# Four and two PSUM banks become three and three: the working ring and the score ring of an attention and mixture-of-experts layer

## The reference: what is computed

```python
x = x + _layernorm(_L0_attn_ref(_layernorm(x), Wq, bq, Wk, bk, Wv, bv))
x = x + _layernorm(_L0_ffn_ref(_layernorm(x), ...))

# attention: 8 blocks of 64 tokens; the first and the last block attend to all,
# block 1 to blocks 0, 1, 2, 7, block 6 to 0, 5, 6, 7,
# the others to block 0, block 7 and themselves with both neighbours
scores = einsum('bhqd,bhkd->bhqk', q, k) * 16 ** -0.5
ctx = einsum('bhqk,bhkd->bhqd', softmax(scores), v)

# feed-forward: a dense branch and 8 experts, the best two of each token
abel_out = gelu(xn @ abel_w + abel_b)
topw, topi = top_k(xn @ moe_gate_w + moe_gate_b, 2)
eo = gelu(xn @ ew1[e] + eb1[e]) @ ew2[e] + eb2[e]
moe_out = (weighted sum of eo) @ expm(gens[0]) @ expm(gens[1]) @ expm(gens[2])
gate = sigmoid(concat(abel_out, moe_out) @ gc_w + gc_b)
out = x + abel_out * (1 - gate) + moe_out * gate
```

## Time and profile before

| | |
|---|---|
| median of three runs | 1788.7 us |
| the profiled execution, its own time | 1799.32 us |
| its span in the profile | 1797.5 us |
| granted TensorE clock, mean | 0.953 of full |
| TensorE (PE) busy | 1543.8 us, 86% |
| weight loads (PEld) busy | 1062.6 us, 59% |
| VectorE (DVE) busy | 1228.8 us, 68% |
| ScalarE (ACT) busy | 898.9 us, 50% |
| GpSimd (POOL) busy | 705.7 us, 39% |
| start of step 3 and of step 15 of `front` | 212.7 us and 940.3 us of the span |

### The profile page before, as it was taken

One profiled execution on the slowest core, in us unless ns is written; L12 is line 12 of the kernel. 1 busy time (PEld: TensorE's weight loads), 2 busy tenths in 40 slices (PEclk: granted clock), 3 DMA queues, 4 the chain that ended last, 5 costly groups with the idle time before them and its releaser, 6 DMA issues. The chain is left out here.

```text
span 1797.5 us, 33500 instructions
## 1 busy us (share of the span) xinstructions
PE 1543.8 (86%) x10385; PEld 1062.6 (59%) x10386; DVE 1228.8 (68%) x3690; ACT 898.9 (50%) x1789; POOL 705.7 (39%) x716
## 2 busy tenths in 40 slices
PE   7889999999999999999999888399999999999500
PEld 5645555545554555455545556288888888888400
DVE  5667787788787878787888633356565665555287
ACT  3146766676667666766776553033333333333244
POOL 1011323442444335333542244144444444544377
PEclk9999999999999999999999989699999999999855
DMA  8132245335533543354334127645656656564397
GB/s 229 36 119 79 88 138 170 119 108 172 160 119 111 177 153 116 123 174 142 123 120 162 52 95 230 191 96 117 134 125 126 134 114 143 105 147 78 48 321 229
DMA packets 186637, 243.59 MB, mean 136 GB/s; under 512 B 23624, under 2 KB 157136, under 8 KB 186384
## 3 DMA queue, kind: packets, MB, share of 16 engines
q1 hardware_dynamic: 159632, 205.67, 36.5%
q0 software_dynamic: 26880, 36.33, 12.4%
HBM read 133.40 MB, written 105.91 MB: 133 GB/s over the span
## 5 line engine op out<-in xcount | busy, mean ns | idle before, releaser
L1053 ACT ACTIVATE pexp<-scT 128x512 f32<-128x512 f32 x768 | 433.6, 598 | 258.7 <-PE scT L839 256.1
L1240 DVE TENSOR_REDUCE mx<-work 128x1 f32<-128x320 f32 (+2 forms) x1024 | 500.6, 547 | 64.3 <-PE work L812 63.7
L1747 POOL DMA_INDIRECT y_rows<-rows_add,row_of x144 | 227.5, 1580 | 298.6 <-DMA y_rows<-rows_add,row_of 235.1
L839 PE MATMUL scT<-w 128*128 128x192 bf16 (+3 forms) x1536 | 282.1, 275 | 26.6 <-ACT pexp L1053 21.8
L812 PE MATMUL work<-w 126*128 126x320 bf16 (+4 forms) x1280 | 269.6, 295 | 31.0 <-DVE mx L1240 27.4
L1779 PE MATMUL h_ps<-inT,w1c 128*128 128x256 f32 x1152 | 263.5, 382 | 2.4 <-DVE inT L1831 2.4
L1792 PE MATMUL o_ps<-w,hT 128*128 x1152 | 260.4, 379 | 0.0
L1722 ACT ACTIVATE rows_add<-rows_out,row_share 128x257 f32<-128x257 f32 x144 | 65.6, 503 | 355.1 <-DVE rows_out L1847 266.3
L1779 PEld LDWEIGHTS h_ps<-inT,w1c 128*128 128x128 f32 x1152 | 220.7, 192 | 33.6 <-issue 3.2
L1792 PEld LDWEIGHTS o_ps<-w,hT 128*128 128x128 f32 x1152 | 213.4, 190 | 26.1
L839 PEld LDWEIGHTS scT<-w 128*128 128x128 bf16 x1536 | 123.5, 97 | 177.6 <-ACT pexp L1053 128.7
(11 more groups left out here) (191 smaller groups left out, 2086.8 us busy)
## 6 DMA issues: line engine op xcount, KB each, us to landing
w<-split_spill SPq DMA_DIRECT2D x384, 128.0 KB, 2.9
split_spill<-split SPq DMA_DIRECT2D x64, 384.0 KB, 3.2
rows_in<-z_rows SPq DMA_DIRECT2D x72, 265.0 KB, 4.8
y_rows<-pre SPq DMA_DIRECT2D x16, 514.0 KB, 5.7
y<-y_rows SPq DMA_DIRECT2D x16, 514.0 KB, 6.7
x_rows<-x SPq DMA_DIRECT2D x16, 512.0 KB, 2.9
abel_rows<-pre SPq DMA_DIRECT2D x16, 512.0 KB, 3.6
abel_in<-abel_rows SPq DMA_DIRECT2D x16, 512.0 KB, 4.4
```

Source lines behind the costliest of these rows:

```text
L839: ins = nc.tensor.matmul(scT[n % 2][:, at:at + hi - lo], tile(kst[par][0:K_EXP, h, :], t), qst[par][0:K_EXP, h, lo:hi], start=True, stop=True)
L1053: nc.scalar.activation(pexp[:, (q * GROUP + n) % NPB, :], scT[n % 2][:, :], ACT.Exp, scale=DH ** -0.5).then_inc(s_exp, 1)
L1240: emptied(nc.vector.reduce_max(mx[:, c:c + 1], bank(s, "max", b, h, t)[:, 0:n], AX_X), s, "max", b, h, t)
L1747: pool.indirect_dma_start(kept.y_rows, bass.IndirectOffsetOnAxis(ap=row_of[n][:, r:r + 1], axis=0), rows_add[n % 2][:, r, :], None, comput ...
```

## The change

The fourth working bank `work3` becomes a third score bank `scT2`. The working ring's items take bank n mod 3 and turn n div 3. Score unit u takes bank u mod 3 (u counts over all batches; 48 units per batch) and waits for the exponential of unit u - 3 in place of u - 2. The exponential reads the same bank. Nothing else changes: each engine has the same instructions in the same order.

```diff
--- before.py
+++ after.py
@@ -331,8 +331,8 @@
         cnt = sb("cnt", [P, 5, NE])
         cnt_i = sb("cnt_i", [P, 2, NE], I32)
 
-        work = [ps(f"work{i}", [P, S]) for i in range(4)]
-        scT = [ps(f"scT{i}", [P, S]) for i in range(2)]
+        work = [ps(f"work{i}", [P, S]) for i in range(3)]
+        scT = [ps(f"scT{i}", [P, S]) for i in range(3)]
         pv = ps("pv", [P, S])
         turn = ps("turn", [P, S])
 
@@ -359,8 +359,8 @@
         s_xn = sem("s_xn")
         s_xt = sem("s_xt")
         s_xnT = sem("s_xnT")
-        w_full = [sem(f"w_full{i}") for i in range(4)]
-        w_free = [sem(f"w_free{i}") for i in range(4)]
+        w_full = [sem(f"w_full{i}") for i in range(3)]
+        w_free = [sem(f"w_free{i}") for i in range(3)]
         s_part1 = sem("s_part1")
         s_part2 = sem("s_part2")
         s_split = sem("s_split")
@@ -506,7 +506,7 @@
 
         AT = {}
         for s_, what_ in [(s_, what_) for s_ in range(B + 3) for what_ in order_of(s_)]:
-            AT[s_, what_] = len(AT) % 4, len(AT) // 4
+            AT[s_, what_] = len(AT) % 3, len(AT) // 3
 
         def bank(s, *what):
 
@@ -834,9 +834,9 @@
                 u = b * UNITS + q * GROUP + n
                 if n == 0 and q in (0, EARLY // GROUP * NCH):
                     pe.wait_ge(s_mrow[int(q > 0)], (b + 1) * N_MAX * 16)
-                wait(pe, s_exp, u - 1)
+                wait(pe, s_exp, u - 2)
                 for t, at, lo, hi in CHUNKS[c]:
-                    ins = nc.tensor.matmul(scT[n % 2][:, at:at + hi - lo],
+                    ins = nc.tensor.matmul(scT[u % 3][:, at:at + hi - lo],
                                            tile(kst[par][0:K_EXP, h, :], t),
                                            qst[par][0:K_EXP, h, lo:hi], start=True, stop=True)
                 ins.then_inc(s_sc, 1)
@@ -1050,7 +1050,7 @@
                 if n == 0:
 
                     wait(act, s_pv, b * QUADS + q - NPB // GROUP + 1)
-                nc.scalar.activation(pexp[:, (q * GROUP + n) % NPB, :], scT[n % 2][:, :], ACT.Exp,
+                nc.scalar.activation(pexp[:, (q * GROUP + n) % NPB, :], scT[u % 3][:, :], ACT.Exp,
                                      scale=DH ** -0.5).then_inc(s_exp, 1)
 
             def evac_ctx(b, g):
```

## The result

The changed kernel takes 1859.2 us (median of four runs, 1856.11 to 1859.84) where the kernel before took 1790.5 beside it: the ratio is 1.0378 (1.036 to 1.0396). A second set of four gave 1856.2 against 1790.8, ratio 1.0358 (1.0337 to 1.0379). So the change costs 65 to 69 us of some 1790.

What follows compares the result with a forecast made beforehand. TensorE, busy 86%, was taken as the bound, held up by ScalarE and VectorE. New waits of 4.7 us less 1.3 removed give 3.4 per step; 13 steps, plus 1.5, less 1, make +45: 1833.4 us, range 1806 to 1854.

Steps and rivals of the forecast that it cites:

- The ring's loss: Waits from giving up the fourth working bank, mostly in projections, values and dense items: 4.7 us new per step.
- P3: Last of a step's four projections; would wait for VectorE's reduction of the second maxima: +1.0 us.
- Z1: Second turned z tile, after the projections; would wait for P3's residual: +1.7 us.
- V0: First value item, after the z tiles; would wait for VectorE's reduction of the fourth maxima: +2.6 us.
- D1: Second dense item, end of quad 1; would start late behind the first dense item: +2.7 us.
- What can stay is 1.3 us per step: Score waits removed by the third score bank: 2.7 us per step, less 1.4 returning as waits for ScalarE's copy.
- The first two steps I put at nothing: Early steps without context work on VectorE; maxima would be read at once, so no loss.
- Quads 3 to 11: Later part of each step: 0.2 us lost entering ScalarE's full stretch, 0.5 in quads 7 to 11, net of score gains.
- the three signs of a wrong mechanism: Step below 61.5 us, V0 within 1 us of its old place, or loss in quads 3 to 11, not before quad 2.
- Faster: Rival: score waits are the real cost and the working ring has slack; about 1760 us, chance 0.08.
- No change: Rival: idle time behind the projections absorbs TensorE's lateness and scores pay the rest; 1789 us, chance 0.08.
- Slower by more: Rival: VectorE fails to catch up, delaying each quad of eight; +1.5 us per step more, 1853 us, chance 0.12.

Runs made afterwards that it cites:

- The runs with short reductions: Each maxima reduction reads 64 keys, exponential scale a thousandth; working and score banks four and two 1738.4 us, three and three 1783.4, three and two 1796.2.
- the kernel with the swap: Changed kernel, with VectorE reducing the second and fourth maxima between the projections before the context tile instead of behind it: 1850.4 us, ratio 1.0336.

## Why the prediction was too low

**The ring's loss: right.** P3 was put at +1.0 and came +1.0, Z1 +1.7 and +1.8, V0 +2.6 and +2.7, D1 +2.7 and +3.1; at D1 the difference is the 0.4 that the scores of quads 0 and 1 were to give back and mostly did not. The releases are those named, read off the rows of VectorE. The ring's gross loss of 4.7 us per step measured 4.8 with the ring changed alone.

**"What can stay is 1.3 us per step": this is the step that failed.** It measured 0.47. I took each wait of a score for an exponential as won, save those in ScalarE's full stretch. These waits were read in the kernel before, and in a kernel with three working banks half of them (11.1 of 21.8 us) are no longer there, since TensorE comes late enough for the exponential. Of the others, TensorE alternates between scores and maxima, and in that kernel the ring of maxima is the shorter one. A score that starts earlier brings its maxima earlier to a bank that VectorE has not read, and the product stays where it was. Two waits that stand in parallel were subtracted as if they stood in series. The runs with short reductions bear this out: with the scores' waits back at 21.7 us and VectorE light, the same bank gives 0.8. (1.3 - 0.47) x 12 = 10 us of the miss.

**"The first two steps I put at nothing": wrong by 5 us.** Step 0 has no context work and no scores, but the products of the matrix exponentials (L716) and 50 maxima units go through the working ring there by turns, each waiting for VectorE: VectorE's own waits for L716 at one line (L1217) rise from 11.1 to 13.5 us, and its waits for the maxima's matmuls (L812) from 2.7 to 4.8; together this is 4.5 of the 5.0 us. The stretch of that step, before, after and with six banks:

```profile
14.07:103.01 88.94, 82.01 (x382) 60.21 (x383) 59.39 (x113) 19.38 (x36) 5.86 (x6) 1.00 0.36 95
```

```profile
14.07:107.99 93.92, 84.35 (x382) 60.21 (x383) 59.93 (x114) 19.45 (x36) 5.87 (x6) 1.00 0.35 90
```

```profile
14.00:95.40 81.40, 78.40 (x382) 60.00 (x383) 58.23 (x111) 19.58 (x36) 5.87 (x6) 1.00 0.38 104
```

The work is the same and the length follows the number of banks: 93.9, 88.9 and 81.4 us with three, four and six working banks, and 84.1 with five (the run of five and one). The prediction worked out no wait of that stretch, though the trace of before has it.

**Quads 3 to 11: right for the ring, wrong for the scores.** I had 0.7 there, it came to 1.3. The ring alone loses 1.7 (the working had 0.5 and 1.1), so the miss is again the scores' share: the 0.3 of quad 5 gave nothing, and the 0.6 of quads 9 and 11 gave 0.35.

**The sum.** 45 predicted; + 10 for the scores' share, + 5 for step 0 gives 60, which is the difference of the traces up to the experts. That the two corrections fill it so exactly is partly chance, since the last row of the table moves by 2.7 us between the two profiles of the kernel before. The medians differ by 65 to 69. Between them lie 5 to 9 us. The stages behind differ by 0.2 us in the first pair of profiles and 1.9 in the second, and their spread of 6 us within one kernel covers the rest; no trace here shows a cause, so this stays open.

**The signs.** The step is 64.95 (64 predicted), VectorE's busy time 50.4 (49.8 predicted), the scores' waits 1.3 us by matmul rows (below 5). L797, L879 and L890 were to wait about 30 us more for VectorE. It is 26: 8.5 + 7.1 + 22.1 = 37.7, against 11.6 before (L890 alone, 8.1 for maxima and 3.5 for values). The gaps themselves came out shorter than said: 0.46 us before P3 (0.5 to 1 predicted), 0.55 before Z1 and 0.65 before V0 (0.9 to 1.5 predicted). Each start is as late as predicted, but it carries the lateness of the one before it. None of the three signs of a wrong mechanism came: the step is not below 61.5, V0 moved by 2.7 us, and 70% of the loss lies before quad 2.

**The rivals.** *Faster* fell with P3's gap. *No change* needed TensorE to catch up in idle time behind the projections; the idle time at the first two dense items grew instead, from 0.84 us to 1.59. *Slower by more* had the size nearly right (1853) but by its own cause, VectorE falling behind in every quad of eight; the value products lose 0.59 us in quads 3 and 4, nothing net in quads 5 and 6 and 0.7 in quads 7 to 11, so this is the smaller part. The rule of the Trainium skill (Perfetto Trace Analysis, Optimization Strategy), that a repeating gap can mean too little PSUM, agrees with the trace of the ring of six, where the gap before the dense items is gone (1.59 us after the change). Taken for the scores alone it would have misled: they had the longest waits, and a bank more gave them 0.47 us per step.

## What to carry to other kernels

When two rings of banks feed one in-order engine, a wait removed in one is worth only what the other ring's next wait leaves of it; follow the engine to the next item that both paths meet in (here the value product) before counting a gain, and do so in the start-up stages too, where the mix of work is another. A bank moved from one ring to another is a trade at the margin: here the third score bank gave 0.5 us per step and the fourth working bank cost 4.8. If two rings peak at different times, one ring over all banks, with each item waiting for whatever last held its bank, can beat a fixed split: here 59.3 us per step against 60.6 (four and two), 64.95 (three and three) and 74 (five and one). Here all that a step gained lay before quad 2, at the projections and dense items, and step 0, which has no scores at all, gained most; that the two rings peak at different times is the likely reason, not a measured one.

## What the runs showed of the hardware

In the kernel with the swap, TensorE waited 1.59 us ahead of the dense items in each of the twelve steps and went on at the full clock in six and at 1.2 GHz for some 3.4 us in the six others, though the busy times ahead agree to 0.01 us in the two stretches shown. In the changed kernel, behind a wait of the same length at the same place, the clock held in all twelve. So a wait can cost more than its own length, and a small gain in one place (1.1 us) can be lost there (1.6 us). What decides between the cases is not shown by these traces.
